# Causal attention: values through stationary tokens, with the probabilities moving and two heads in halves of the columns

## The chip, the cores and the metric

One core of a Trainium2 chip runs the whole computation as one program. The metric is the time of one execution on the device in microseconds, lower is better.

## The reference

The input x is 4 batches of 64 channels by 32x32 positions, so 1024 tokens of 64 channels a batch, all fp32.

```python
# 1. attention over positions with 32 channels, softmax over all 1024 keys, and a residual
att = softmax(einsum('bmi,bmj->bij', k, q)); x = x + wo @ (att @ v)
# 2. causal attention with 8 heads of width 64 on t = tokens(x), after a layer norm, and a residual
scores = q @ k.T / 8 ; scores[above the diagonal] = -1e30
t = t + concat_heads(softmax(scores) @ (ln(t) @ Wv)) @ Wo
# 3. a recurrence over the 1024 tokens, on batch-normalised W @ ln(t), and a residual
y[t] = sigmoid(wx[t] + V @ y[t-1]);  t = t + y
```

The change is in part 2 alone.

## The kernel before

**Units and items.** Part 1 is 4 units (one a batch), part 2 is 16 units of two heads (4 batches by 4 pairs of heads). A unit of part 2 has 9 pairs of items, `ATTN_RUNS`; the two items of a pair are the two heads. An item is 512 columns of transposed scores: keys of one 128-token tile on the partitions, queries in the columns, in one or two runs `(key tile, first query tile, query tiles, place)`. The 9 pairs cover the lower triangle of the causal matrix: pairs 1, 2 and 8 have two runs, the others one. Eight blocks of a unit lie on the diagonal and need the mask: one in pairs 0 and 7, two in pairs 1, 2 and 8.

**One item.** TensorE makes the scores of both heads, each on 64 rows of the array, as three fp16 products (keys and queries are split into a high and a low fp16 part), into one of 3 PSUM banks a head (`ST`). ACT writes exp of them as fp32 (`probs`, ring of 10) and, for a split item, once more as fp16 (`probs_high`). POOL subtracts for `probs_low`. Three pairs later TensorE multiplies with the values: the 128x128 block of probabilities is stationary and 65 columns of values move (64 channels of the projected output and a one, which sums the denominator). A split item takes three fp16 products for each block (L574, L576, L578), a whole item one fp32 product (L570). Every sixth item is whole (`ATTN_WHOLE`), 3 of 18.

**Values and scale.** The values are tokens times a matrix of Wv and Wo, so a product with them gives the head's share of the output at once. Each unit computes them in two "values" steps: 8 small products each, two ACT casts, one DVE subtraction. When a half of the queries (4 tiles) of a head is complete, DVE takes the reciprocal of the denominators (L979) and scales (L983), and POOL adds to the tokens (L1260): 4 times a unit.

**Row maxima.** The scores are made shift-free by the row maxima of a cheaper score (high parts alone), computed one unit ahead: one product a head and step (L497), masks by a product of an identity and a mask (L483), a DVE reduction (L903), a transpose, a negation (L927) and a DMA into the queries' first row.

**Order.** Every engine is in order and walks the same slots: item i is scored in slot i, and its pair in an even slot. Value products come `LAG` = 6 slots later, that is three pairs. Within a slot TensorE does value products, then the auxiliary products of the slot (`AUXES`: queries, values, max transpose, keys), then masks, maxima and scores. DVE does scales, reductions, then the subtractions of the auxiliary products, then pieces of layer norms. From slot 64 on all auxiliary products use one PSUM bank, and the maxima two (one a head), so each waits for the user before it. Scores of a pair wait until the first head of the pair before has both its exponentials. Layer norms of a batch run on POOL (`pool_ln1`, L1286 to L1291, with Newton steps L1271 to L1274 ahead) at fixed slots.

## Time and profile before

| | |
|---|---|
| median of 3 runs | 571.24 us |
| lowest and highest | 567.42 and 571.98 us |
| profiled execution, first to last instruction | 567.0 us |
| PE, DVE, ACT, POOL busy | 490.0, 398.8, 429.3, 424.4 us |
| mean granted TensorE clock | 0.974 |

The profile is one execution, seen by the hardware profiler; its span lies 0.4 us under the lowest of the three runs. Busy time of PE counts each matmul with its latency, so close matmuls overlap in it. "Idle before" is the time in which an engine stood still ahead of an instruction, with what ended it.

### The profile page before, as it was taken

The numbers are of one execution on the slowest core, as the hardware profiler recorded it, in microseconds if no ns is written. First come the engines' busy times: TensorE is split into PE (matmuls) and PEld (weight loads), VectorE is DVE, ScalarE is ACT, GpSimd is POOL, SyncE is SP. The second block draws the span as 40 slices with busy tenths as digits, with TensorE's granted clock in tenths as the row PEclk, the third lists the DMA queues.
The fourth block names the chain that finished last, engine by engine and source line by source line (L and its number), as shares of the span: only waits on it lengthen the run. The fifth ranks groups of instructions, "written<-read, shape, count | busy, mean of one in ns | idle before, by whom it ended". The sixth has DMA issues, their size and how long they took to land.

```text
span 567.0 us, 16744 instructions
## 1 busy us (share of the span) xinstructions
PE 490.0 (86%) x6771; PEld 323.0 (57%) x6771; DVE 398.8 (70%) x909; ACT 429.3 (76%) x832; POOL 424.4 (75%) x463
## 2 busy tenths in 40 slices
PE   4699978988799998889999988998999999787783
PEld 1277655655565755565666756565666766564431
DVE  5878888767678786576767676766767786328757
ACT  3488867866778878587888878787888878785593
POOL 3867965857988797968788797899788799985002
PEclk9999999989999999799999999999999999998698
DMA  9100000000000000000000000000000000000001
GB/s 230 68 3 2 2 20 1 4 1 3 1 22 2 3 3 2 3 1 21 2 3 2 4 3 1 21 3 1 1 3 3 2 3 2 2 2 2 0 2 74
DMA packets 3580, 7.46 MB, mean 13 GB/s; under 512 B 1168, under 2 KB 1456, under 8 KB 3376
## 3 DMA queue, kind: packets, MB, share of 16 engines
q1 hardware_dynamic: 3056, 5.34, 3.5%
q8 instruction: 54, 0.88, 0.7%
q10 hardware_dynamic: 448, 1.05, 0.6%
q14 instruction: 22, 0.18, 0.1%
HBM read 4.22 MB, written 1.05 MB: 9 GB/s over the span
## 4 chain that ended last, share of the span: by engine, by line
PE 45%; DVE 22%; POOL 17%; ACT 9%; issue 6%; DMA 1%; DVEq 0%; SPq 0%; POOLq 0%; ACTq 0%
POOL probs_low L1250 10%; PE bank L537 9%; DVE attn_partial_max L903 7%; ACT probs_high L779 6%; PE bank L497 6%; PE bank L570 5%; PE bank L574 4%; DVE conv_partial_max L897 3%; PE bank L578 3%; PE bank L576 3%; PE bank L455 2%; PE bank L522 2%; PE bank L483 2%; PE bank L456 2%; POOL tokens L1260 2%
## 5 line engine op out<-in xcount | busy, mean ns | idle before, releaser
L1250 POOL TENSOR_TENSOR probs_low<-probs,probs_high 128x512 f16<-128x512 f32 x288 | 327.6, 1158 | 77.5 <-ACT probs_high L779 76.7
L775 ACT ACTIVATE probs<-bank 128x512 f32<-128x512 f32 x352 | 214.7, 611 | 84.2 <-PE bank L537 69.0
L903 DVE TENSOR_REDUCE attn_partial_max<-bank 128x1 f32<-128x512 f32 (+2 forms) x288 | 185.3, 685 | 99.5 <-PE bank L497 99.0
L779 ACT ACTIVATE probs_high<-bank 128x512 f16<-128x512 f32 x288 | 176.8, 614 | 0.0
L574 PEld LDWEIGHTS bank<-values_high,probs_high 128*128 128x128 f16 x1152 | 105.7, 98 | 74.2 <-issue 35.8
L574 PE MATMUL bank<-values_high,probs_high 128*128 128x65 f16 x1152 | 128.8, 196 | 15.5 <-POOL probs_low L1250 11.4
L576 PE MATMUL bank<-values_low,probs_high 128*128 128x64 f16 x1152 | 127.6, 194 | 0.0
L578 PE MATMUL bank<-values_high,probs_low 128*128 128x65 f16 x1152 | 127.1, 194 | 0.0
L576 PEld LDWEIGHTS bank<-values_low,probs_high 128*128 128x128 f16 x1152 | 106.9, 99 | 3.2
L578 PEld LDWEIGHTS bank<-values_high,probs_low 128*128 128x128 f16 x1152 | 107.2, 98 | 0.0
L570 PE MATMUL bank<-values,probs 128*128 128x65 f32 x512 | 71.7, 278 | 0.8 <-POOL probs_low L1250 0.8
L570 PEld LDWEIGHTS bank<-values,probs 128*128 128x128 f32 x512 | 64.7, 192 | 3.5 <-POOL probs_low L1250 1.0
L497 PE MATMUL bank<-attn_keys_high,queries_high 64*128 64x512 f16 (+3 forms) x384 | 56.7, 332 | 7.9 <-ACT probs_high L779 6.0
L1260 POOL TENSOR_TENSOR tokens<-scaled_outputs,tokens 128x256 f32<-128x256 f32 x71 | 51.7, 729 | 8.0 <-DVE scaled_outputs L983 3.3
L537 PE MATMUL bank<-queries_high,attn_keys_high 64*128 64x512 f16 (+3 forms) x384 | 55.6, 326 | 1.1 <-ACT probs_high L779 1.1
L537 PE MATMUL bank<-queries_high,attn_keys_low 64*128 64x512 f16 (+3 forms) x384 | 55.5, 325 | 0.0
L537 PE MATMUL bank<-queries_low,attn_keys_high 64*128 64x512 f16 (+3 forms) x384 | 55.5, 325 | 0.0
L897 DVE TENSOR_REDUCE conv_partial_max<-bank 128x1 f32<-128x512 f32 x64 | 42.8, 687 | 5.8 <-PE bank L470 4.7
L983 DVE TENSOR_TENSOR scaled_outputs<-bank,reciprocal_denominators 128x256 f32<-128x256 f32 x72 | 30.6, 425 | 7.6 <-DVE reciprocal_denominators L979 0.5
L522 PE MATMUL bank<-causal_masks,identity_bf 128*128 128x128 bf16 x256 | 27.5, 219 | 6.6 <-ACT probs_high L779 6.4
L497 PEld LDWEIGHTS bank<-attn_keys_high,queries_high 64*128 64x128 f16 x384 | 15.3, 93 | 29.7 <-issue 6.8
L1343 POOL TENSOR_TENSOR x_split<-probs 128x512 f32<-128x512 f32 x4 | 4.2, 1092 | 36.1 <-ACT probs L878 36.1
(192 smaller groups left out, 708.9 us busy)
## 6 DMA issues: line engine op xcount, KB each, us to landing
x_channels<-in_x_cm SPq DMA_DIRECT2D x6, 256.0 KB, 7.6
tokens<-in_x_tm SPq DMA_DIRECT2D x1, 1024.0 KB, 10.4
out<-ln_channels SPq DMA_DIRECT2D x4, 256.0 KB, 2.0
attn_weights<-in_attn_w ACTq DMA_DIRECT2D x1, 512.0 KB, 6.2
attn_keys_split<-attn_keys_high SPq DMA_DIRECT2D x4, 128.0 KB, 2.3
attn_keys_split<-attn_keys_low SPq DMA_DIRECT2D x4, 128.0 KB, 2.4
queries_high<-minus_max_rows SPq DMA_DIRECT2D x32, 2.0 KB
x_channels<-in_x_cm ACTq DMA_DIRECT2D x2, 128.0 KB, 3.2
```

Source lines behind the costliest of these rows:

```text
L497: last[r] = nc.tensor.matmul(prep_bank(m + r)[:, at * P:(at + tiles) * P], q[rows(r), t * P:(t + 1) * P], xs_hi[rows(r), b * N + j0 * P:b ...
L537: last[r] = nc.tensor.matmul(ST[(i + r) % ST_RING][:, at * P:(at + tiles) * P], keys[rows(r), b * N + j * P:b * N + (j + 1) * P], queries[ ...
L570: ins = nc.tensor.matmul(dst, e32[:, item % E_RING, cols], v32[v % 2][:, j, r, :], start=opens, stop=True, skip_group_check=True)
L574: nc.tensor.matmul(dst, hi, v_hi[v % 2][:, j, r, :], start=opens, stop=False, skip_group_check=True)
L576: nc.tensor.matmul(dst[:, 0:C], hi, v_lo[v % 2][:, j, r, :], start=False, stop=False, skip_group_check=True)
L578: ins = nc.tensor.matmul(dst, lo, v_hi[v % 2][:, j, r, :], start=False, stop=True, skip_group_check=True)
L775: ins = nc.scalar.activation(e32[:, i % E_RING, :], o[:], ACT.Exp, scale=scale)
L779: ins = nc.scalar.activation(p_hi[:, i % P_RING, :], o[:], ACT.Exp, scale=scale)
L897: nc.vector.reduce_max(cmx[v % 2][:, t, part:part + 1], o[:], AX).then_inc(s_prep_used, 1)
L903: nc.vector.reduce_max(dst, o[:].rearrange("p (n w) -> p n w", n=n), AX).then_inc(s_prep_used, 1)
L1250: nc.gpsimd.tensor_tensor(out=p_lo[:, i % P_RING, :], in0=e32[:, i % E_RING, :], in1=p_hi[:, i % P_RING, :], op=ALU.subtract).then_inc(s_r ...
L1260: nc.gpsimd.tensor_tensor(out=dst, in0=scaled[:, half % S_RING, :, :], in1=dst, op=ALU.add).then_inc(s_added, 1)
```

## The change

The value products change sides. Tokens after the layer norm (`xh`, 64 channels, the first replaced by a one) are stationary, 64 columns for each head, and the probabilities move, up to 512 columns at once. Head 0 writes partitions 0 to 63 of the bank and head 1 partitions 64 to 127 (`sums_bank`): halves of the array's columns. So the products give sums of tokens, not of values. When a half of the queries is complete, ACT casts the sums of both heads to fp16 (`o_hi`), DVE subtracts (`o_lo`), and an auxiliary step "outputs" for each head multiplies them with the value matrix: four tiles of three products, with 64 rows. DVE scales from its bank as before. The "values" steps are gone.

Pairs 3 to 6 are split in fp16; pairs 0, 1, 2, 7 and 8 are whole, for both heads. All masked blocks are in whole pairs; they are now set to zero after the exponential by POOL (`pool_mask`, `affine_select` on the two heads' 128 columns at once), and the score masks on TensorE are gone. The masks of the maxima stay, as two products over half the rows each. Layer-norm steps on POOL get a cast and a subtraction for the tokens' fp16 parts and move by some slots.

```diff
-CONV_WHOLE, ATTN_WHOLE = 4, 6
+CONV_WHOLE = 4
+SPLIT_PAIRS = (3, 4, 5, 6)
...
-ATTN_MAXT_SLOT, ATTN_VALUES_SLOTS = -4, (-2, 2)
+ATTN_MAXT_SLOT, OUTPUT_SLOTS, LAST_OUTPUT_SLOTS = -4, (12, 16, 24, 28), (12, 14, 24, 25)
...
-LN1_APPLY_SLOT = (23, 80, 136, 214)
-KEY_SLOTS = ((32, 34), (88, 92), (154, 160), (226, 232))
+LN1_APPLY_SLOT = (23, 80, 144, 216)
+KEY_SLOTS = ((32, 34), (89, 93), (157, 161), (227, 231))
...
+        def pe_sums(i):
+            v = unit_of(i)
+            b = batch_of(v)
+            if not whole(i):
+                nc.tensor.wait_ge(s_rest, rests(i + 1))
+            elif diagonals(i):
+                nc.tensor.wait_ge(s_masked, masked(i))
+            else:
+                nc.tensor.wait_ge(s_probs, i + 2)
+            last = [None, None]
+            for j, t0, tiles, at in runs_of(i):
+                c = t0 // TPC
+                opens = (v, c) not in OPENED
+                if opens:
+                    OPENED.add((v, c))
+                    if v > B:
+                        nc.tensor.wait_ge(s_sums, 2 * (v - B - 1) + c + 1)
...
+                if whole(i):
+                    products = ((xh[b % 2][:, j, 0, :], e32, E_RING),)
+                else:
+                    x_hi, x_lo = xh_hi[b % 2][:, j, :], xh_lo[b % 2][:, j, :]
+                    products = ((x_hi, p_hi, P_RING), (x_lo, p_hi, P_RING), (x_hi, p_lo, P_RING))
+                for n, (x, p, ring) in enumerate(products):
+                    for r in range(2):
+                        last[r] = nc.tensor.matmul(sums_bank(c)[rows(r), cols], x, p[:, (i + r) % ring, src],
+                                                   start=opens and n == 0, stop=n == len(products) - 1,
+                                                   skip_group_check=True)
...
+            elif what == "outputs":
+                n, r = k // 2, k % 2
+                h = 2 * (n // NC % PAIRS) + r
+                nc.tensor.wait_ge(s_sums, n + 1)
+                for t in range(TPC):
+                    o, cols = bank[:, t * PO:(t + 1) * PO], slice(t * P, (t + 1) * P)
+                    hi, lo = o_hi[n % 2][rows(r), cols], o_lo[n % 2][rows(r), cols]
+                    nc.tensor.matmul(o, hi, pr_hi[rows(r), h, :], start=True, stop=False, skip_group_check=True)
+                    nc.tensor.matmul(o[:, 0:C], hi, pr_lo[rows(r), h, :], start=False, stop=False,
+                                     skip_group_check=True)
+                    ins = nc.tensor.matmul(o, lo, pr_hi[rows(r), h, :], start=False, stop=True,
+                                           skip_group_check=True)
...
+        def act_sums(n):
+            v, c = B + n // NC, n % NC
+            nc.scalar.wait_ge(s_values, closed_by(v, c) + 1)
+            if n >= 2:
+                nc.scalar.wait_ge(s_aux, AUX_OF["outputs", 2 * (n - 2) + 1] + 1)
+            nc.scalar.activation(o_hi[n % 2][:], sums_bank(c)[:], ACT.Copy).then_inc(s_sums_cast, 1)
...
+        def dve_sums(n):
+            nc.vector.wait_ge(s_sums_cast, n + 1)
+            nc.vector.tensor_tensor(out=o_lo[n % 2][:], in0=sums_bank(n % NC)[:], in1=o_hi[n % 2][:],
+                                    op=ALU.subtract).then_inc(s_sums, 1)
...
+        def pool_mask(i):
+            nc.gpsimd.wait_ge(s_probs, i + 2)
+            for at in diagonals(i):
+                e = e32[:, i % E_RING:i % E_RING + 2, at * P:(at + 1) * P]
+                nc.gpsimd.affine_select(out=e, in_=e, pattern=[[0, 2], [1, P]], compare_op=ALU.is_ge, fill=0.0, base=0,
+                                        channel_multiplier=-1).then_inc(s_masked, 1)
```

How the order moves on TensorE, in a late unit, around the queries products and the scores of pair 2. Before, with the values of two items of the pair three steps earlier ahead of them:

```order
L574 MATMUL bank<-values_high,probs_high 128x65
L576 MATMUL bank<-values_low,probs_high 128x64
L578 MATMUL bank<-values_high,probs_low 128x65
...
L570 MATMUL bank<-values,probs 128x65 x4
L455 MATMUL bank<-attn_keys_split,qk_matrix_high 128x512
L456 MATMUL bank<-attn_keys_split,qk_matrix_low 128x512
L522 MATMUL bank<-causal_masks,identity_bf 128x128 x4
L497 MATMUL bank<-attn_keys_high,queries_high 128x512 x2
L537 MATMUL bank<-queries_high,attn_keys_high 128x256 x4
```

Now, the same place and what follows up to the next maxima:

```order
L600 MATMUL bank<-probs,ln_out 64x384 x2
L600 MATMUL bank<-probs,ln_out 64x128 x2
L460 MATMUL bank<-attn_keys_split,qk_matrix_high 128x512
L461 MATMUL bank<-attn_keys_split,qk_matrix_low 128x512
L506 MATMUL bank<-attn_keys_high,queries_high 128x512 x2
L535 MATMUL bank<-queries_high,attn_keys_high 128x256 x4
...
L600 MATMUL bank<-probs,ln_out 64x512 x2
L659 MATMUL bank<-value_matrix_high,sums_high 128x65
L660 MATMUL bank<-value_matrix_low,sums_high 128x64
L662 MATMUL bank<-value_matrix_high,sums_low 128x65
...
L506 MATMUL bank<-attn_keys_high,queries_high 128x512 x2
```

The value products went from 65 to up to 512 moving columns and from one head at a time to two side by side, the score masks (L522) went, and in the next step the outputs stand between the sums and the maxima.

DVE, steps 2 to 6 of a late unit (reductions are of the maxima, `queries_low` are the subtractions of the queries steps). Before:

```order
L903 TENSOR_REDUCE attn_partial_max<-bank 128x4 x2
L959 TENSOR_TENSOR values_low<-bank,values_high 128x512
L979 RECIPROCAL reciprocal_denominators<-bank 128x4
L983 TENSOR_TENSOR scaled_outputs<-bank,reciprocal_denominators 128x256
L979 RECIPROCAL reciprocal_denominators<-bank 128x4
L983 TENSOR_TENSOR scaled_outputs<-bank,reciprocal_denominators 128x256
L903 TENSOR_REDUCE attn_partial_max<-bank 128x1 x2
L964 TENSOR_TENSOR queries_low<-bank,queries_high 128x512
L903 TENSOR_REDUCE attn_partial_max<-bank 128x1 x4
```

Now:

```order
L937 TENSOR_REDUCE attn_partial_max<-bank 128x1 x2
L1026 TENSOR_TENSOR sums_low<-bank,sums_high 128x512
L994 TENSOR_TENSOR queries_low<-bank,queries_high 128x512
L1008 RECIPROCAL reciprocal_denominators<-bank 128x4
L1012 TENSOR_TENSOR scaled_outputs<-bank,reciprocal_denominators 128x256
L937 TENSOR_REDUCE attn_partial_max<-bank 128x1 x4
L994 TENSOR_TENSOR queries_low<-bank,queries_high 128x512
L1008 RECIPROCAL reciprocal_denominators<-bank 128x4
L1012 TENSOR_TENSOR scaled_outputs<-bank,reciprocal_denominators 128x256
L937 TENSOR_REDUCE attn_partial_max<-bank 128x1 x2
L943 TENSOR_REDUCE row_max<-attn_partial_max 128x2x4 x2
L1026 TENSOR_TENSOR sums_low<-bank,sums_high 128x512
```

The two scales of a half no longer stand together, and each subtraction of sums comes behind the reductions of its slot.

POOL, one unit. Before:

```order
L1250 TENSOR_TENSOR probs_low<-probs,probs_high 128x512 x10
L1260 TENSOR_TENSOR tokens<-scaled_outputs,tokens 128x4x64 x2
L1250 TENSOR_TENSOR probs_low<-probs,probs_high 128x512 x5
L1260 TENSOR_TENSOR tokens<-scaled_outputs,tokens 128x4x64 x2
```

Now:

```order
L1299 TENSOR_TENSOR probs_low<-probs,probs_high 128x512 x4
L1321 TENSOR_TENSOR tokens<-scaled_outputs,tokens 128x4x64
L1299 TENSOR_TENSOR probs_low<-probs,probs_high 128x512 x2
L1321 TENSOR_TENSOR tokens<-scaled_outputs,tokens 128x4x64
L1307 AFFINE_SELECT probs<-probs 128x2x128 x3
L1321 TENSOR_TENSOR tokens<-scaled_outputs,tokens 128x4x64
L1307 AFFINE_SELECT probs<-probs 128x2x128 x5
```

Of 15 low parts 8 are left, and 8 masks came.

## Rows read from the trace of the kernel before

**Rows 1.** The page, section 1: busy us (share of the span) and instructions.

```profile
PE 490.0 (86%) x6771; PEld 323.0 (57%) x6771; DVE 398.8 (70%) x909; ACT 429.3 (76%) x832; POOL 424.4 (75%) x463
```

**Rows 2.** Groups by line, whole span: count, busy, mean ns, idle; one instruction.

```profile
L1250 POOL TENSOR_TENSOR probs_low<-probs,probs_high 128x512 f16<-128x512 f32 x288 | 327.6, 1158 | 77.5 <-ACT probs_high L779 76.7
L1260 POOL TENSOR_TENSOR tokens<-scaled_outputs,tokens 128x256 f32<-128x256 f32 x71 | 51.7, 729 | 8.0 <-DVE scaled_outputs L983 3.3 <-POOL tokens L1260 0.4
...
L927 DVE TENSOR_SCALAR minus_max_rows<-bank x16: 269/279/279, 105.9 to 489.2; 16x128 f16<-16x128 f32 x16
```

**Rows 3.** PE timeline, 409 to 425 us: start, length, count, [idle].

```profile
415.18 0.38 PE L537 MATMUL bank<-queries_high,attn_keys_high 64*128 64x512 f16 x2
...
424.12 0.20 PE L574 MATMUL bank<-values_high,probs_high 128*128 128x65 f16 x1
...
424.86 0.22 PE L455 MATMUL bank<-value_matrix_high,attn_keys_split 128*128 128x128 f16 x1
```

**Rows 4.** PE's timeline, 425 to 441 us.

```profile
425.30 0.39 PE L483 MATMUL bank<-causal_masks,identity_bf 128*128 128x128 bf16 x4
425.52 0.39 PE L522 MATMUL bank<-causal_masks,identity_bf 128*128 128x128 bf16 x4
425.84 0.39 PE L497 MATMUL bank<-attn_keys_high,queries_high 64*128 64x128 f16 x4
426.07 0.38 PE L537 MATMUL bank<-queries_high,attn_keys_high 64*128 64x384 f16 x4
426.29 0.38 PE L537 MATMUL bank<-queries_low,attn_keys_high 64*128 64x384 f16 x4
...
426.82 0.20 PE L574 MATMUL bank<-values_high,probs_high 128*128 128x65 f16 x1
...
427.20 1.08 PE L570 MATMUL bank<-values,probs 128*128 128x65 f32 x8
428.21 0.39 PE L455 MATMUL bank<-attn_keys_split,qk_matrix_high 128*128 128x512 f16 x1
...
431.28 0.39 PE L497 MATMUL bank<-attn_keys_high,queries_high 64*128 64x512 f16 x2 [0.43 <-ACT probs_high L779]
...
438.87 0.38 PE L537 MATMUL bank<-queries_high,attn_keys_high 64*128 64x512 f16 x2
```

**Rows 5.** ACT's timeline, 425 to 441 us.

```profile
430.05 0.60 ACT L775 ACTIVATE probs<-bank 128x512 f32<-128x512 f32 x1 [0.34 <-PE bank L537]
430.55 0.59 ACT L779 ACTIVATE probs_high<-bank 128x512 f16<-128x512 f32 x1
```

**Rows 6.** DVE timeline, 216 to 262 us; PE timeline (last row).

```profile
242.92 1.29 DVE L903 TENSOR_REDUCE attn_partial_max<-bank 128x2 f32<-128x512 f32 x2 [1.68 <-PE bank L497]
244.12 0.68 DVE L959 TENSOR_TENSOR values_low<-bank,values_high 128x512 f16<-128x512 f32 x1
...
251.76 0.18 DVE L979 RECIPROCAL reciprocal_denominators<-bank 128x4 f32<-128x4 f32 x1
...
252.38 0.17 DVE L979 RECIPROCAL reciprocal_denominators<-bank 128x4 f32<-128x4 f32 x1
...
244.86 0.66 PE L651 MATMUL bank<-constants,ln_out 128*128 128x128 f32 x4 [0.56 <-DVE values_low L959]
```

**Rows 7.** PE's weight loads, 553 to 567 us.

```profile
555.63 0.19 PEld L752 LDWEIGHTS bank<-probs,ffn_weights 128*128 128x128 f32 x1 [0.24 <-ACT probs L875]
556.05 0.19 PEld L752 LDWEIGHTS bank<-probs,ffn_weights 128*128 128x128 f32 x1 [0.24 <-issue]
```

**Rows 8.** POOL groups and timeline, 205 to 262 us; PE waits.

```profile
L1303 POOL CAST causal_masks<-constants 128x256 bf16<-128x256 f32 x1 | 0.4, 397 | 0.0
...
L1291 POOL COPY ln_out<-ln_out 128x512 f32<-128x512 f32 x4 | 2.4, 611 | 0.3
...
227.12 2.27 POOL L1250 TENSOR_TENSOR probs_low<-probs,probs_high 128x512 f16<-128x512 f32 x2
...
PE bank L574 <- POOL probs_low L1250: 3.4, 2, 3.1
```

More of the change, by code:

```diff
@@ L471, in pe_conv_prep, with pe_mask @@
                              start=True, stop=True).then_inc(s_prep, 1)
+        def pe_mask(blocks, opens):
+            for half in range(2):
+                for r in range(2):
+                    nc.tensor.matmul(blocks[r], masks[rows(r), half, 0, :], masks[rows(r), half, 1, :],
+                                     start=opens and half == 0, stop=False, skip_group_check=True)
         def pe_max_masks(m):
             _, v, k = PREPS[m]
+            if v == B and k == 0:
+                nc.tensor.wait_ge(s_masks, 32)
             for r in range(2):
                 pe_wait_bank(BANK_HAD["prep", m + r])
[L478 to L485 removed]
+            ends = [(at + tiles) * P for t, j0, tiles, at in ATTN_MAXES[k // 2][0] if j0 + tiles - 1 == t]
+            for n, end in enumerate(ends):
+                pe_mask([prep_bank(m + r)[:, end - P:end] for r in range(2)], n == 0)
         def pe_maxes(m):
@@ L839, in _ @@
                     act_aux(m)
+                for n in SUMS_AT.get(g, ()):
+                    act_sums(n)
                 for i in items_at(g):
@@ L1101, in _ @@
             for g in range(FIRST_SLOT, LAST_SLOT):
-                for half in HALVES_AT.get(g, ()):
-                    dve_scale(half)
+                for half in CONV_HALVES_AT.get(g, ()):
+                    dve_conv_scale(half)
                 for m in auxes_at(g):
@@ L1120, in _ @@
                         dve_rowmax(v)
+                for n in SUMS_AT.get(g, ()):
+                    dve_sums(n)
                 for m in auxes_at(g):
@@ L1359, in _ @@
             sp.dma_start(gbt[:], gb).then_inc(s_ffn, 16)
+            sp.wait_ge(s_init, 2)
+            for r in range(2):
+                sp.dma_start(masks[rows(r), 1, :, :], masks[rows(1 - r), 0, :, :]).then_inc(s_masks, 16)
             for m, (_, _, what, k) in enumerate(AUXES):
```

272 lines of the change are left out of this document (129 added, 143 removed).

## The prediction, made before the changed kernel ran

> **What bounds the kernel now.** I read the page first, then one undisturbed unit in the timelines of PE, ACT and DVE, then the waits. The page [rows 1] has PE at 86% and no engine much behind, but a busy PE here counts the latency tail of every matmul, so the answer lies in the steps. I number the nine steps of a unit 0 to 8: step n computes the row maxima for the next unit, the scores of item pair n, and the value products of pair n-3 (of the unit before where n is below 3).
>
> One unit takes 23.69 us, from the scores at 415.18 to the same ones at 438.87 [rows 3, 4]. The whole sequence of 16 units is slower: the max rows, one per unit, stand at 105.9 and 489.2 [rows 2], 25.55 us apart on average, so 15 intervals carry 15 x (25.55 - 23.69) = 28 us of disturbance. Part of it are bursts of POOL work for a layer norm: behind one, after which the low parts go on at 227.12, PE had waited twice for a low part, up to 3.1 us [rows 8].
>
> Inside a unit two things alternate. Where a step has extra products PE simply works through: from the value products at 424.12 over the aux products at 424.86, masks and maxima to the next scores at 426.07 there is no idle time [rows 3, 4]. In plain steps a loop of latencies sets the pace: ACT starts the first head's exponential at 430.05, its fp16 copy at 430.55, which ends at 431.14, and PE, idle for 0.43 us, starts at 431.28 [rows 4, 5]. By the prices below a unit has nine steps of 1.10, values 8.6, queries and values aux 2.0, masks 1.8 and a transpose, together some 22 us of PE work, and under 2 us of such waiting.
>
> **Prices on PE** [rows 3, 4]. A product of 512 columns for both heads, each on its own half of the rows: 426.07 to 426.29, 0.22 us, the two together, since both are through in 0.39 us with the latency (scores: three such, 0.65; maxima: 0.23). A causal mask block for both heads: 0.11 us (two blocks of the maxima from 425.30 to 425.52). A change of shape costs 0.10 us from scores to values (426.07 + 0.65 = 426.72, then 426.82) and some 0.10 to 0.14 back (425.52 + 0.22 = 425.74, then 425.84). Split values of a pair: 24 matmuls of 65 columns, 424.12 to 424.86, 0.74 us, or 0.031 each. A whole item of one head: four fp32 products of 65 columns in eight passes, from 427.20 to the next product at 428.21, 1.0. So a unit's values cost 7.5 x 0.74 + 3 x 1.0 = 8.6 us now. A 512-column fp32 product is two passes, whose weight loads start at 555.63 and 556.05: 0.43 us a pass [rows 7].
>
> **The change part by part.**
> Removed from PE: the score masks, 8 blocks x 0.11 = 0.9 us a unit, and the values aux, 2 x 0.44 (424.86 to 425.30) = 0.9. Added: four outputs aux of 12 matmuls x 0.031 = 0.37, with their start 0.39 each, 1.6 us a unit. The max masks are now two half-height products for each head, side by side: 0.11 us a block, unchanged.
> The value products themselves: a split pair becomes three fp16 products of 512 columns for two heads, which lie in halves of the array's columns. No row shows column halves at once. If they overlap as the row halves do, 3 x 0.22 = 0.65 us (now 0.74); if not, 1.3. A whole pair is one fp32 product for each head, and each is two passes. In program order these are head 0 first pass, head 0 second, head 1 first, head 1 second. The second can't start before the first has left the same half; the third can run beside the second; the fourth waits for the third. That is three pass times, 1.29 us; with two runs of 384 and 128 columns 1.17, of 256 and 256 1.07. Bounds: 0.86 if the heads overlap wholly, 1.72 if not at all. I take three passes because every row of PE's timeline starts in program order. The Trainium skill, page "TensorE: Matmul & The Clock Gate", section Part 3, says that matmuls start and end strictly in program order whatever tile they are on. By that rule 1.29 stands and 0.86 falls, which agrees with the order of the starts in this trace.
>
> PE work of a unit after the change: nine steps x 1.10 (scores 0.65, maxima 0.23, shape 0.22) = 9.9; split sums 4 x 0.65 = 2.6; whole sums 2 x 1.29 + 2 x 1.17 + 1.07 = 6.0; queries 2 x 0.57 (two products and one more change of shape) = 1.1; outputs 1.6; max masks 0.9; max transpose 0.15. Sum 22.2 us, as much as now. So PE gains nothing: what the masks and the values aux give back, the outputs and the fp32 passes take.
>
> ACT: 15 items of a unit had a second exponential for the fp16 copy, 8 keep it; 4 value casts go and 2 casts of sums come: 9 activations fewer. At 0.50 us from start to start [rows 5] that is 4.5 us less in a unit. It shortens the loop of latencies (the wait of 0.43 us), but most steps are longer than the loop now, so what is late next is PE itself, and DVE.
>
> POOL: 15 low parts x 1.16 = 17.4 us become 8 x 1.16 = 9.3; the four additions of 0.73 stay [rows 2]. Added are 8 masks of 128x256 in fp32. None is in the trace. Nearest below: a cast of the same size, 0.40 us; nearest above: the low part of 128x512, 1.16 [rows 2, 8]. I take 0.6, near the one-input copy of 512 columns at 0.61. POOL then holds 9.3 + 2.9 + 4.8 = 17 us of a unit, and 21.5 at the upper end: hidden under 24.6 in both cases. It isn't late in the steps either: a mask has three steps before its sums.
>
> DVE: the values-low subtraction turns into one of the sums, 2 x 0.68 for 2 x 0.68, but it now stands between PE and PE. The chain is sums on PE, cast on ACT, subtraction on DVE, outputs on PE, with one step for all of it. DVE does in a step, counted from the start of the maxima: +0.42 first reduce (the maxima's latency; 242.92 in rows 6), two reduces to +1.62 (244.12 - 242.92 = 1.20), each further subtraction 0.60 from start to start and 0.68 to its end; PE starts 0.06 us after that end (244.12 + 0.68 = 244.80, then 244.86) [rows 6]. A scale of one half, reciprocal to next reciprocal, is 251.76 to 252.38, 0.62 us.
> - Step 2 has the sums' and the queries' subtraction: DVE is done at +2.90. PE asks for the bank at step 3 after 0.23 + 0.65 + 0.10 + 1.29 + 0.12 = +2.39. Wait with the start: 0.6 us.
> - Step 4 has the queries' subtraction: +2.37 against +2.17 at step 5. Wait 0.2.
> - Step 5 has the scale of an output ahead of the reduces (they end at +1.99), the two row maxima and then the sums' subtraction, which ends at +2.98; PE asks at step 6 after a split pair, +1.75. Wait 1.3 us. Queued behind it on PE are a mask, the maxima and the scores of step 6, so ACT and DVE get their work later by the same 1.3.
> - Steps 7 and 0 find the two maxima banks still being reduced, since an output's scale went first: 0.1 and 0.15.
> Together 2.35 us, and 22.2 + 2.35 = 24.6 us for a unit, +0.9 on 23.69.
>
> Outside the steady unit: the burst of POOL for a layer norm gains a cast and a subtraction, some 1.7 us (0.6 + 1.16), and moves to step 4, between low parts that PE needs; but POOL has slack in the other steps, and the burst of the third norm falls into mask steps. I put the 28 us at 24. The last unit has no maxima, so no DVE waits, and fewer low parts at its end: -1.5. After the last sums, a cast (0.60) and a subtraction (0.68) and the outputs stand ahead of the scale: +2. The masks' exchange by two DMAs on SP lies at the start of the program, 80 us and more ahead of its first use in part 2; queued behind it is only the first row of maxima of part 1, which isn't ready by then: nothing.
>
> Sum against the profiled execution: 567.0 + 15 x 0.9 - 4 - 1.5 + 2 = 577. The profile is the length of the fastest of three runs (567.4), and their median is 571.2; I add 2 and say 579.
>
> **The rivals.**
> A, the heads overlap wholly in fp32 too (0.86 for a whole pair). Steps 1, 2 and 4 get 0.43, 0.32 and 0.32 shorter; steps 3 and 5 don't, since DVE sets them then (+2.90 and +2.37). A unit is 23.5, and the sum 567.0 - 3 - 4 - 2.5 + 2 = 559.5, so 561. Against it: two passes of one product follow each other in one place.
> B, column halves don't overlap in fp32: 1.72 for a whole pair. Steps 1, 2, 4, 5 grow by 0.43, 0.54, 0.54, 0.44, step 3 is covered by the DVE wait: 26.5 a unit, 577 + 15 x 1.95 = 606, so 608. If fp16 halves don't overlap either, +1.7 a unit more. Decided by whether a second head's pass starts before the first head's ends. The Trainium skill, same page and section, has weight loads overlap running matmuls only when their row group differs, or into a background buffer; column halves share all rows. By the first half of that rule B would be the case; the trace has full-height loads 0.031 us apart under running matmuls, which speaks for the background buffer.
> C, the mask costs POOL far more than a copy. POOL is the bound from (24.6 - 12.2) / 8 = 1.55 us a mask; at 2.3, twice the upper row, a unit is 12.2 + 18.4 = 30.6 and the time 577 + 90 = 667. No row speaks for it; the operation is simply unseen.
> D, the disturbances go with POOL's load: of the 28 us only 10 stay. Then 577 - 14 = 563, so 565. For it: POOL has 7 us less in a unit. Against it: the bursts grow and stand between low parts.
>
> **How the numbers follow.** Forecast 0.42, A 0.25, B 0.15, C 0.08, D 0.10. About 1% is what a measurement of this kernel can tell from no change (its three runs lie 0.8% apart). Faster by over 1% (below 565.5): most of A (0.18), half of D (0.06), the low edge of the forecast (0.03): 0.27. Slower by over 1% (above 577): 0.26 of the forecast, B and C: 0.49. Within: 0.24. The forecast alone reaches from 571 to 588. The range leaves out C, most of B's upper half and the bottom of D with A: 554 to 606.
>
> **What would show each step.** A unit's period, from scores to the same scores: 24.6 (A 23.5, B 26.5). Four fp32 passes of a whole pair within 1.3 us. PE idle ahead of the outputs' products at step 6 for 1.3 us, released by the sums' low part on DVE, and at step 3 for 0.6. POOL below 75% busy with masks of about 0.6 us. ACT at some 60%. The prediction is wrong if passes of the two heads start together, if a column half's weights are waited for, or if the long steps around the layer norms go.

## The result, and the profile after

| | before | after |
|---|---|---|
| median of the runs | 570.7 us (4 runs) | 581.7 us (4 runs, 579.2 to 583.0) |
| profiled execution, first to last instruction | 567.0 us | 578.6 us |
| mean granted TensorE clock | 0.974 | 0.953 |

The ratio is 1.020 with an interval of 1.016 to 1.024: the changed kernel is slower by 2%. The page's busy line and the groups that answer to [rows 1, 2, 8] (busy time and mean ns of one; then idle time ahead, with what ended it):

```profile
PE 468.0 (81%) x4915; PEld 235.2 (41%) x4915; DVE 397.5 (69%) x912; ACT 359.6 (62%) x688; POOL 352.1 (61%) x487
...
L1299 POOL TENSOR_TENSOR probs_low<-probs,probs_high 128x512 f16<-128x512 f32 x176 | 200.0, 1157 | 79.0 <-ACT probs_high L809 77.8
...
L1307 POOL TENSOR_SCALAR_AFFINE_SELECT probs<-probs 128x256 f32<-128x256 f32 x128 | 49.6, 407 | 81.2 <-ACT probs L805 80.9
L600 PE MATMUL bank<-probs,ln_out 128*64 128x384 f32 (+3 forms) x512 | 88.4, 456 | 5.0 <-POOL probs L1307 5.0
```

PE, ACT and POOL all have less busy time than before, DVE nearly the same, and the kernel is longer: no engine's load explains it. The mask costs 0.407 us, as much as the cast of its size.

Next, one late undisturbed unit in PE's timeline (start, length, engine, line, operands; in brackets the idle time ahead). It answers to [rows 3, 4]:

```profile
435.66 1.08 PE L600 MATMUL bank<-probs,ln_out 128*64 128x512 f32 x4
436.67 0.40 PE L482 MATMUL bank<-identity_and_causal_mask 64*128 64x128 bf16 x8
...
442.39 0.20 PE L659 MATMUL bank<-value_matrix_high,sums_high 64*128 64x65 f16 x1 [0.91 <-DVE queries_low L994]
...
447.63 0.20 PE L659 MATMUL bank<-value_matrix_high,sums_high 64*128 64x65 f16 x1 [0.32 <-DVE queries_low L994]
...
449.07 0.41 PE L600 MATMUL bank<-probs_high,ln_out_high 128*64 128x512 f16 x2
449.31 0.38 PE L600 MATMUL bank<-probs_high,ln_out_low 128*64 128x512 f16 x2
449.53 0.38 PE L600 MATMUL bank<-probs_low,ln_out_high 128*64 128x512 f16 x2
...
451.17 0.19 PE L659 MATMUL bank<-value_matrix_high,sums_high 64*128 64x65 f16 x1 [1.26 <-DVE sums_low L1026]
```

A whole pair, four fp32 passes (x4), is over after 1.08 us, latency included, and the next product starts after 1.01: two pass times, not three. Unmerged, the first passes of the two heads start at 435.657 and 435.664, the second at 436.137 and 436.144. The waits for DVE are there, 0.91, 0.32 and 1.26 us. The unit, from the first scores to the same ones, takes 23.68 us, exactly as long as before (23.69).

So the 11.6 us lie outside the steady unit. This table is worked out from the first scores products of each of the 16 units in the two timelines:

| us | before | after |
|---|---|---|
| start to the first scores of part 2 | 111.15 | 112.10 |
| 15 intervals, less 15 steady ones | 29.0 | 38.2 |
| last unit | 18.7 | 15.9 |
| from its last scores to the end | 52.8 | 57.2 |
| units 1, 4, 8, 11 (steady is 23.7) | 27.2, 29.5, 26.0, 23.7 | 34.5, 32.0, 27.4, 28.0 |

Unit 4 shows what a long unit is. On POOL (first fence) the block of operations for one layer norm, the burst, runs from Newton steps to L1355 ahead of the low parts; on PE (second fence) the product behind that wait:

```profile
234.80 0.23 POOL L1332 TENSOR_TENSOR newton_scratch<-ln_rstd,ln_var_eps 128x16 f32<-128x16 f32 x1
...
238.40 1.05 POOL L1348 TENSOR_TENSOR ln_out<-tokens,ln_mean_var 128x512 f32<-128x512 f32 x1
239.53 1.04 POOL L1350 TENSOR_TENSOR ln_out<-ln_out,ln_rstd 128x512 f32<-128x512 f32 x1
240.63 0.11 POOL L1352 MEMSET ln_out<- 128x8 f32 x1
240.80 0.61 POOL L1353 COPY ln_out<-ln_out 128x512 f32<-128x512 f32 x1
241.47 0.61 POOL L1354 CAST ln_out_high<-ln_out 128x512 f16<-128x512 f32 x1
242.17 1.15 POOL L1355 TENSOR_TENSOR ln_out_low<-ln_out,ln_out_high 128x512 f16<-128x512 f32 x1
243.28 2.26 POOL L1299 TENSOR_TENSOR probs_low<-probs,probs_high 128x512 f16<-128x512 f32 x2
```

```profile
245.59 0.64 PE L600 MATMUL bank<-probs_high,ln_out_high 128*64 128x512 f16 x2 [5.87 <-POOL probs_low L1299]
246.02 0.64 PE L600 MATMUL bank<-probs_high,ln_out_low 128*64 128x512 f16 x2
```

The burst is 8.5 us in one piece (234.80 to 243.3), and the two low parts behind it end at 245.54. PE had stood for 5.87 us by then, and its next products start 0.43 us apart instead of 0.24: it runs at the lower of its two clock levels (1.2 GHz). The granted clock is the last column but two in these rows, of a stretch before the wait and one behind it:

```profile
236.00:239.00 3.00, 2.86 (x45) 1.61 (x44) 2.08 (x5) 1.62 (x4) 2.34 (x9) 1.00 0.00 0
245.50:250.00 4.50, 4.41 (x44) 2.81 (x46) 1.65 (x4) 0.07 (x1) 3.99 (x6) 0.50 0.03 5
```

Before, the burst of this layer norm was 6.6 us (220.53 to 227.12) and PE's longest wait behind it 3.1. The burst in unit 8 has no Newton steps: 4.9 us (341.97 to 346.86), and PE waits 2.29.

The clock is a second cost of such waits. In the 15 intervals PE stands at the lower level for 27.3 us, 10.2 before. The run with the burst in three parts, below, has a unit that shows the price: its unit 2 has the program of the run before it and the same idle time of PE (3.4 us), but 6.8 us at the lower level and not none, and takes 27.6 us against 24.7. That is 0.43 us for each us at the lower level. Unit 11 of the changed kernel, with 3.4 us of it, is 1.65 us longer than with none in the last run below; unit 1, with 10.2, is 1.9 us longer than with 3.4 in the run with slots 141 and 213, whose program is the same up to there. By these rates (0.28 to 0.49) the 17 us more at the lower level are worth 5 to 8 of the 9.2 us by which the intervals grew, an estimate.

### The profile page after: what moved, and what is told of

The parts are those of the page before. It is cut to its first block, busy times and chain, and to the rows that moved or that the text cites. A ratio compares the mean times of both kernels' runs of the same rounds, so it can differ in the third digit from the quotient of the medians.

```text
span 578.6 us, 12934 instructions
## 1 busy us (share of the span) xinstructions
PE 468.0 (81%) x4915; PEld 235.2 (41%) x4915; DVE 397.5 (69%) x912; ACT 359.6 (62%) x688; POOL 352.1 (61%) x487
## 4 chain that ended last, share of the span: by engine, by line
PE 44%; DVE 33%; POOL 13%; issue 5%; ACT 4%; DMA 1%; DVEq 0%; SPq 0%; POOLq 0%; ACTq 0%
DVE attn_partial_max L937 13%; PE bank L600 11%; PE bank L535 8%; POOL probs_low L1299 6%; PE bank L506 5%; DVE conv_partial_max L931 3%; DVE queries_low L994 3%; DVE sums_low L1026 3%; DVE scaled_outputs L1012 2%; PE bank L482 2%; PE bank L659 2%; PE bank L460 2%; PE bank L559 2%; PE bank L461 1%; ACT probs_high L809 1%
## 5 line engine op out<-in xcount | busy, mean ns | idle before, releaser
L1299 POOL TENSOR_TENSOR probs_low<-probs,probs_high 128x512 f16<-128x512 f32 x176 | 200.0, 1157 | 79.0 <-ACT probs_high L809 77.8
L809 ACT ACTIVATE probs_high<-bank 128x512 f16<-128x512 f32 x176 | 107.4, 610 | 0.0
L1307 POOL TENSOR_SCALAR_AFFINE_SELECT probs<-probs 128x256 f32<-128x256 f32 x128 | 49.6, 407 | 81.2 <-ACT probs L805 80.9
L600 PE MATMUL bank<-probs,ln_out 128*64 128x384 f32 (+3 forms) x512 | 88.4, 456 | 5.0 <-POOL probs L1307 5.0
L659 PE MATMUL bank<-value_matrix_high,sums_high 64*128 64x65 f16 x256 | 30.8, 195 | 39.4 <-DVE sums_low L1026 22.4
L600 PEld LDWEIGHTS bank<-probs,ln_out 128*64 128x64 f32 x512 | 29.9, 137 | 46.9 <-issue 31.5
L600 PE MATMUL bank<-probs_high,ln_out_high 128*64 128x512 f16 x128 | 27.2, 421 | 12.0 <-POOL probs_low L1299 12.0
L482 PE MATMUL bank<-identity_and_causal_mask 64*128 64x128 bf16 x512 | 32.6, 221 | 2.4 <-DVE attn_partial_max L937 1.6
L506 PEld LDWEIGHTS bank<-attn_keys_high,queries_high 64*128 64x128 f16 x384 | 22.0, 95 | 25.6 <-DVE attn_partial_max L937 13.5
L660 PE MATMUL bank<-value_matrix_low,sums_high 64*128 64x64 f16 x256 | 30.4, 192 | 0.0
L662 PE MATMUL bank<-value_matrix_high,sums_low 64*128 64x65 f16 x256 | 30.4, 193 | 0.0
```

The costliest lines, as they stand in the source:

```text
L482: nc.tensor.matmul(blocks[r], masks[rows(r), half, 0, :], masks[rows(r), half, 1, :], start=opens and half == 0, stop=False, skip_group_ch ...
L506: last[r] = nc.tensor.matmul(prep_bank(m + r)[:, at * P:(at + tiles) * P], q[rows(r), t * P:(t + 1) * P], xs_hi[rows(r), b * N + j0 * P:b ...
L600: last[r] = nc.tensor.matmul(sums_bank(c)[rows(r), cols], x, p[:, (i + r) % ring, src], start=opens and n == 0, stop=n == len(products) - ...
L659: nc.tensor.matmul(o, hi, pr_hi[rows(r), h, :], start=True, stop=False, skip_group_check=True)
L809: ins = nc.scalar.activation(p_hi[:, i % P_RING, :], o[:], ACT.Exp, scale=scale)
L1299: nc.gpsimd.tensor_tensor(out=p_lo[:, i % P_RING, :], in0=e32[:, i % E_RING, :], in1=p_hi[:, i % P_RING, :], op=ALU.subtract).then_inc(s_r ...
```

## Experiments

All of them start from the changed kernel unless another base is named. Ratios are to the kernel before, timed beside them (medians 569.5 to 570.5 us). "Disturbance" is the table's second line, what 15 intervals take over 15 steady units.

**Full width in fp32.** The stationary tokens of whole pairs are 128 columns wide, so the two heads' products use the same columns.

```diff
+                if whole(i):
+                    x = xh[b % 2][:, j, :, :].rearrange("p a c -> p (a c)")
+                    for r in range(2):
+                        last[r] = nc.tensor.matmul(sums_bank(c)[:, cols], x, e32[:, (i + r) % E_RING, src], ...)
```

> The changed kernel with the stationary tokens of a whole pair taken 128 columns wide (both copies), so that each head's fp32 product fills the whole array and the heads can't run side by side. It leaves the two heads' sums of whole pairs added together in both halves, so the outputs are not those of the reference; the number of products and columns streamed is unchanged. Theory (the trace of the changed kernel: passes of the two heads start 7 ns apart, so 0.86 us for a whole pair): four passes in a row, 1.72 us a whole pair; steps 1, 2 and 4 grow by 0.86, step 5 by 0.54 (0.32 of it hides behind DVE), step 3 by nothing (the wait of 0.91 us for DVE covers it). Steady unit 23.68 + 3.1 = 26.8 us, profiled execution near 578.6 + 46 = 625 us. Rival (the value products are not what PE is bound by in these steps): under 600 us.

Measured: 622.5 us, one run; steady unit 26.74. A whole pair on PE:

```profile
464.80 1.99 PE L601 MATMUL bank<-probs,ln_out 128*128 128x512 f32 x4
```

Four passes now take 1.99 us with latency against 1.08. With nothing side by side the unit is 3.05 us longer, close to what rival B's sum gave (26.5 a unit). In the changed kernel the heads do overlap.

**Split products one head after the other.** The three products of head 0, then the three of head 1, in program order.

```diff
-                for n, (x, p, ring) in enumerate(products):
-                    for r in range(2):
+                for r in range(2):
+                    for n, (x, p, ring) in enumerate(products):
```

> The changed kernel with the three fp16 products of a split pair issued for one head and then for the other, not alternating; whole pairs are issued as before. It tells how a pass that can't start holds up one of the other half behind it. If products start strictly in program order (the step of the prediction that gave three pass times for a whole pair), the second product of head 0 holds up head 1: 5 x 0.22 = 1.08 us for a split pair in place of 0.65, step 6 unchanged behind its DVE wait, steps 7, 8 and 0 longer by 0.3 to 0.43: steady unit 24.8, profiled execution near 578.6 + 17 = 596 us. If PE looks ahead and starts head 1's products as soon as its half is free, as the fp32 passes of the changed kernel may show: 0.65 us, no change within 2 us.

Measured: 580.7 us, one run; steady unit 23.69. The same pair as above:

```profile
449.15 0.41 PE L600 MATMUL bank<-probs_high,ln_out_high 128*64 128x512 f16 x2
449.39 0.39 PE L600 MATMUL bank<-probs_high,ln_out_low 128*64 128x512 f16 x2
449.61 0.39 PE L600 MATMUL bank<-probs_low,ln_out_high 128*64 128x512 f16 x2
```

Each line still holds one product of each head (x2) and is no longer than a single one. Head 1's first product, fourth in the program, starts with head 0's first and ahead of head 0's second. The unit and the profiled execution (578.8 us) are those of the changed kernel. So PE doesn't hold a product on one column half behind those of the other half that stand earlier in the program. That is the premise on which the prediction chose three passes, and it is wrong here. The Trainium skill, page "TensorE: Matmul & The Clock Gate", section Part 3, has matmuls start and end strictly in program order; this trace shows otherwise for column halves.

**Outputs at odd slots.** The outputs' steps move by one slot, so that DVE's subtraction of the sums has one step more.

```diff
-ATTN_MAXT_SLOT, OUTPUT_SLOTS, LAST_OUTPUT_SLOTS = -4, (12, 16, 24, 28), (12, 14, 24, 25)
+ATTN_MAXT_SLOT, OUTPUT_SLOTS, LAST_OUTPUT_SLOTS = -4, (13, 17, 25, 29), (12, 14, 24, 25)
```

> The changed kernel with the four outputs steps of a unit one slot later (13, 17, 25, 29 in place of 12, 16, 24, 28), so that they come behind the maxima and scores of their step and ahead of the next sums, and DVE scales outside the reductions' way. Theory (the waits for the sums' and queries' subtraction are real costs of the changed order, 0.91 + 0.32 + 1.26 = 2.5 us in each steady unit): most of them go, a steady unit is 21.3 to 22 us instead of 23.68, and the time some 15 x 2 = 30 us lower, ratio to the changed kernel about 0.95. Rival (the chain over DVE is late wherever PE asks, and the wait only moves to the sums or the max transpose behind it): steady unit within 0.5 us of 23.68, under 8 us in all.

Measured: 574.0 us, ratio 1.007 (1.004 to 1.009). The steady unit is 21.88, so the waits for DVE were real and cost 1.80 us a unit. But the disturbance grew from 38 to 58 us, so most of the 27 us was given back. The list of waits, first of the changed kernel, then with odd slots (total, times, longest):

```profile
PE bank L659 <- DVE sums_low L1026: 22.4, 17, 3.1
PE bank L659 <- DVE queries_low L994: 13.8, 23, 1.0
PE bank L600 <- POOL probs_low L1299: 12.0, 5, 5.9
```

```profile
PE bank L600 <- POOL probs_low L1299: 14.4, 5, 7.3
...
PE bank L638 <- DVE scaled_outputs L1012: 11.6, 13, 2.4
...
PE bank L460 <- DVE scaled_outputs L1012: 5.1, 9, 1.6
...
PE bank L680 <- DVE scaled_outputs L1012: 4.5, 3, 1.9
...
PE bank L659 <- DVE sums_low L1026: 3.1, 1, 3.1
```

The waits for the sums' subtraction are gone but for 3.1 us, those for the queries' are 3.9 in the 15 intervals. The wait for low parts grew by 2.4 us alone. New are the waits for DVE's scale ahead of the max transposes (L638), the queries (L460), the keys (L680) and the outputs: together 24.3 us in the 15 intervals, 0.78 in each steady one. Units without a burst lost most: units 2 and 3 rose from 24.0 and 24.5 to 26.0 and 26.6, with 3.1 and 3.7 us of this wait and 3.4 us each at the lower clock level. Units 1, 4 and 8, where low parts or masks wait for the burst, fell by 1.6, 1.3 and 0.3. So the bursts took a part of what the outputs saved, and new waits for DVE and the clock took more. No run parts the two.

**The burst at other slots.** First, slots 144 and 216 go to 141 and 213, right behind the masks of pair 2.

```diff
-LN1_APPLY_SLOT = (23, 80, 144, 216)
+LN1_APPLY_SLOT = (23, 80, 141, 213)
```

> The changed kernel with POOL's layer-norm bursts of batches 2 and 3 at slots 141 and 213 in place of 144 and 216, ahead of the four split pairs and not among them. Theory (the disturbances are POOL bursts of 8.3 and 4.5 us that stand between low parts, behind which PE waited 5.9 us): low parts start late but later steps catch up, the wait gets 2 to 3 us shorter for batch 2 and 2 us for batch 3: 3 to 5 us in all. Rival (the burst costs its whole surplus wherever it stands, since POOL has no slack before the split pairs): within 1 us of the changed kernel, or slower.

Measured: 576.5 us, ratio 1.009 (1.006 to 1.013); units 4 and 8 at 29.4 and 23.8 (32.0 and 27.4). The 5.2 us are at the top of what the theory expected, but 1.9 of them lie in unit 1, which the edit doesn't touch (it has less time at the lower clock level), and unit 9 rose from 26.6 to 27.7. Then behind the mask of pair 7, `(23, 79, 151, 223)`:

> Base: the changed kernel (581.7 us). POOL's bursts for the layer norms of batches 1, 2 and 3 move from slots 80, 144, 216 to 79, 151, 223, just behind the single mask of pair 7, so that only masks stand behind them, the first of which is wanted four steps later. Theory 'the burst is late where low parts or masks of the next three steps stand behind it': the burst of 8.3 us fits into four steps (some 10 us) with its masks, so the long units of the changed kernel, 34.45 (unit 1), 31.97 (unit 4) and 27.37 (unit 8), lose most of what lies over 23.7 to 24.6 that isn't due to other work: unit 4 to some 24.5 (-7.5), unit 8 to 24 (-3.5), unit 1 (moved by one slot only) by 1 to 2; whole time 568 to 572. Rival 'POOL has no room for a burst in any 24 us stretch (15 of its own and 8.3)': a wait of equal length comes up elsewhere, and the time stays within 3 us of the 576.5 of the kernel with slots 141 and 213.

Measured: 578.5 us, ratio 1.013 (1.009 to 1.017). Units 4 and 8 fall to 24.0 and 23.7 as expected, but units 5 and 9 rise to 32.8 and 31.0: the time is the rival's. My theory had left out one user of the burst:

```profile
249.54 1.08 PE L680 MATMUL bank<-constants,ln_out 128*128 128x128 f32 x4 [3.82 <-POOL ln_out_low L1355]
```

These are the transposes for the keys of the next batch, which in units 5 and 9 stand at step 1 or 0. The wait had only moved. With odd outputs on top:

> The run before (bursts at 79, 151, 223) and the outputs at odd slots (13, 17, 25, 29) together. Odd slots alone took the steady unit from 23.68 to 21.88, but the sequence of 15 intervals gained only 8 us and not 27, because units with a burst or layer-norm work grew. Theory 'the two add up': steady unit 21.88, disturbances those of the run before; 15 x 1.8 = 27 us less than it, whole time some 545. Rival 'with shorter units POOL and DVE, which have the same work to do in less time, take it back': each burst (8.3 us of POOL beside 15 us of its own) makes a unit at least 23.3, each unit with 16 tiles of statistics on DVE stays at 25 or more: some 560 to 565.

Measured: 569.7 us, ratio 0.998 (0.995 to 1.001): steady 21.88, disturbance 50. Against the late bursts alone odd outputs gave 9 us, not 27, and the rival's 560 to 565 was too low as well. It was right that the time is taken back; how much of it by POOL and how much by DVE is open.

**The tail.** In the last unit alone pairs 5 and 6 are whole too.

```diff
-    return ... else n // 2 not in SPLIT_PAIRS
+    return ... else n // 2 not in SPLIT_PAIRS[:2 if unit_of(i) == UNITS - 1 else 4]
```

> Base: the changed kernel. In the last unit alone pairs 5 and 6 are whole in fp32 too, so POOL has four low parts fewer (4 x 1.16 us) just before the end, and ACT four copies fewer. Theory 'the longer tail (57.2 us from the last scores to the end, before 52.8) is made by low parts ahead of the additions on POOL, for which DVE's last statistics wait, and behind which the subtraction of the last sums stands on DVE': the addition comes some 2.3 to 3 us sooner, the subtraction starts when the cast is done, the tail is some 54, whole time 2 to 4 us less (578 to 580). Rival 'the tail is the added chain of cast, subtraction and outputs alone': it stays at 57 and the time within 1 us; the two pairs cost PE 0.2 us each more in fp32.

Measured: 581.2 us, ratio 1.019 (1.015 to 1.022): no difference to be told. DVE's timeline of the changed kernel near the end, then with this edit:

```profile
525.29 0.61 DVE L1115 BATCH_NORM_STATS2 ln_stats<-tokens 128x6 f32<-128x64 f32 x4 [4.68 <-POOL tokens L1321]
...
529.37 0.68 DVE L1026 TENSOR_TENSOR sums_low<-bank,sums_high 128x512 f16<-128x512 f32 x1
```

```profile
523.61 0.61 DVE L1115 BATCH_NORM_STATS2 ln_stats<-tokens 128x6 f32<-128x64 f32 x4 [2.13 <-POOL tokens L1321]
...
527.79 0.68 DVE L1026 TENSOR_TENSOR sums_low<-bank,sums_high 128x512 f16<-128x512 f32 x1
```

The last sums' subtraction stands behind 4 us of statistics on DVE, and those wait for an addition on POOL that stands behind low parts. Fewer low parts bring both forward, until the mask ahead of the addition sets it, for which POOL waits 1.65 us for ACT: the tail is 55.8 us instead of 57.2. That part of the theory is seen in the trace, but 1.4 us is less than half of what I expected and below what the three rounds can tell.

**All moves together**: late bursts, odd outputs, the last unit, and the second projection for part 3 out of unit 11.

```diff
-LN3_TRANSPOSE_SLOTS, WX_SLOTS = (257, 263), (261, 267)
+LN3_TRANSPOSE_SLOTS, WX_SLOTS = (257, 263), (261, 281)
```

> All moves together: bursts at 79, 151, 223, outputs at odd slots, the second of the two projections of the layer-norm tokens of part 3 from slot 267 to 281 (between the two queries steps it had waited 1.9 us for DVE in unit 11), and pairs 5 and 6 of the last unit whole. By the theory that each move acts in its own place: the time of the run with late bursts and odd slots less 3 to 4 us for unit 11 (27.97 us in the changed kernel) and 2 to 4 for the tail, 540 if those two add up, and under the kernel before (570.5) by 5%. By the rival that POOL and DVE take it back: 555 to 560, under it by 2 to 3%.

Measured: 565.0 us, ratio 0.990 (0.987 to 0.993). Unit 11 goes from 25.1 to 22.5 and unit 12 from 21.9 to 22.9: 1.6 us from the projection. The time misses both expectations (540, and 555 to 560). Units 1, 5 and 9, with the keys behind the burst, still take 31.2, 32.8 and 32.2.

**Keys later.** Base: all moves.

```diff
-KEY_SLOTS = ((32, 34), (89, 93), (157, 161), (227, 231))
+KEY_SLOTS = ((32, 34), (91, 97), (163, 169), (235, 241))
```

> Base: the run with all moves (565.0 us). There a burst of POOL of 8 to 10 us was still followed by one wait of PE of the same kind, now for the tokens after the norm: the transposes for the keys of the next batch stood at step 1 of the following unit (slots 89, 157, 227), the trace has PE idle for 3.8 to 4.9 us ahead of them, and step 1 or 0 of units 1, 5 and 9 at 6.84, 10.02 and 8.11 us. Here the keys steps of batches 1 to 3 move from (89, 93), (157, 161), (227, 231) to (91, 97), (163, 169), (235, 241). Theory 'the keys alone held the late burst': unit 1 31.2 to 27, unit 5 32.8 to 26, unit 9 32.2 to 26; 4 + 6 + 6 = 16 us less, whole time 547 to 551, 4% under the kernel before. Rival 'POOL has no room': masks or low parts behind the burst are late instead, and the time stays over 560.

Measured: 558.4 us, ratio 0.979 (0.976 to 0.982). 7 us of the 16: unit 9 lost 3.8, unit 3 1.5, unit 1 1.0, unit 5 nothing (32.9). What took the keys' place:

```profile
143.93 1.98 PE L600 MATMUL bank<-probs,ln_out 128*64 128x384 f32 x8 [3.66 <-POOL probs L1307]
...
247.76 1.98 PE L600 MATMUL bank<-probs,ln_out 128*64 128x384 f32 x8 [5.52 <-POOL probs L1307]
...
342.74 1.08 PE L600 MATMUL bank<-probs,ln_out 128*64 128x384 f32 x8 [1.93 <-POOL probs L1307]
```

Now the masks of pair 8 were late. The rival of this run ("masks or low parts behind the burst are late instead") had the mechanism, though the time fell to 558; neither range holds it. The same with the outputs at even slots:

> The run with late keys, but with the outputs back at the changed kernel's slots (12, 16, 24, 28). In the changed kernel the odd slots gained 1.80 us in a steady unit and only some 8 us over all of 15 intervals. Theory 'the rest was hidden behind waits for the bursts and for the keys, which set those units whatever the outputs do': with these waits gone odd slots are worth more, some 15 to 20 us, and this run takes 565 to 570. Rival 'units with layer-norm work on DVE can't gain from odd slots at all': the difference stays at 8 to 9 us, and this run takes 556 to 560.

Measured: 574.0 us, ratio 1.006 (1.004 to 1.008). Odd outputs are now worth 15.6 us, where they were worth 8 and 9. The difference is within the theory's 15 to 20, the time above both its range and the rival's. In the units with a burst or keys (1, 4, 5, 8, 9) odd outputs saved 3.1 us in all on the changed kernel and 8.7 here: so much had been hidden. Another 2.7 us come from units 2 and 3, which here have no time at the lower clock level. Some 11 of the 27 us stay lost, with 21.5 us of waits for DVE's scale in the intervals.

**The burst in three parts.** Base: keys later. The same instructions, with other POOL work between; the Newton steps of batch 2 also come 12 slots sooner (batch 3 has none).

```diff
-LN1_APPLY_SLOT = (23, 79, 151, 223)
+LN1_PART_SLOTS = ((23, 23, 23), (79, 81, 85), (139, 153, 157), (211, 225, 229))
...
-                    if g == LN1_APPLY_SLOT[b]:
-                        pool_ln1(b)
+                    for part in range(3):
+                        if g == LN1_PART_SLOTS[b][part]:
+                            pool_ln1(b, part)
```

> Base: the run with late keys (558.4 us). In it the burst of one layer norm, 8.5 us in one piece, still holds PE at step 1 of units 1, 5 and 9 (7.75, 9.63, 5.15 us, PE idle 3.66, 5.52 and 1.93 us ahead of the sums of pair 8, for its masks). In every placement so far (slots 80/144/216, 141/213, 79/151/223) some product of PE waited 4 to 6 us for what stood behind the piece. Here the same instructions run in three parts with masks and low parts between: Newton steps (3.6 us) at slots 79, 139, 211, the two operations of the norm (2.3 us) at 81, 153, 225, copy, cast and low part (2.5 us) at 85, 157, 229. Theory 'one piece of 8 us exceeds the slack of a mask or low part (three steps, 7 us, less the time POOL is behind), parts under 4 us don't': units 1, 5 and 9 lose their waits, 30.2 to 26.5, 32.9 to 27.3, 28.4 to 26.5, and whole time is some 11 us less, 547. Rival 'POOL has no room in these units (15 us of its own, 8.5 of burst, units of 22 to 24)': the waits spread over several steps, the three units stay at 29 or more, and the time stays over 555.

Measured: 545.4 us, ratio 0.956 (0.953 to 0.958). Units 1, 5, 9 are at 24.5, 25.8 and 25.8 (30.2, 32.9, 28.4). Units 2 and 3 rose, from 24.7 and 25.1 to 27.6 and 26.6, with the same waits but 6.8 and 3.4 us at the lower clock level. Unit 2, the run before and this one:

```profile
167.43:192.14 24.71, 21.27 (x239) 9.73 (x239) 19.80 (x52) 15.58 (x30) 14.77 (x21) 1.00 0.04 10
```

```profile
162.85:190.47 27.62, 24.20 (x239) 10.43 (x238) 19.80 (x52) 15.66 (x30) 14.77 (x21) 0.88 0.04 9
```

POOL's timeline at the second and third part, where masks (L1307) run between them:

```profile
239.60 1.05 POOL L1357 TENSOR_TENSOR ln_out<-tokens,ln_mean_var 128x512 f32<-128x512 f32 x1
240.73 1.04 POOL L1359 TENSOR_TENSOR ln_out<-ln_out,ln_rstd 128x512 f32<-128x512 f32 x1
241.84 0.11 POOL L1361 MEMSET ln_out<- 128x8 f32 x1
242.02 0.41 POOL L1307 TENSOR_SCALAR_AFFINE_SELECT probs<-probs 128x256 f32<-128x256 f32 x1
...
243.23 0.77 POOL L1307 TENSOR_SCALAR_AFFINE_SELECT probs<-probs 128x256 f32<-128x256 f32 x2
243.95 0.61 POOL L1348 COPY ln_out<-ln_out 128x512 f32<-128x512 f32 x1
```

In this run's list of waits PE waits for masks no more, and for low parts of part 2 for 3.5 us in all:

```profile
PE bank L600 <- POOL probs_low L1299: 3.5, 3, 1.5
```

Last, parts and late keys alone on the changed kernel:

> The changed kernel (581.7 us) with nothing but the three parts of the burst (slots 79/81/85, 139/153/157, 211/225/229) and, which they need, the late keys (91, 97), (163, 169), (235, 241); outputs, projections and last unit as in the changed kernel. Theory 'the burst in one piece made most of what the changed kernel's sequence lost over its steady unit': units 1, 4, 5, 8 and 9 go from 34.45, 31.97, 27.83, 27.37, 26.61 to some 27, 24, 27, 23.7, 27 (what is left is the keys' own work of some 3 us), 19 us less, whole time 562 to 564, under the kernel before (570) by 1 to 1.5%. Rival 'the parts only paid together with odd outputs, whose waits stood in the same steps': units 5 and 9 keep 29 or more, whole time over 569.

Measured: 566.0 us, ratio 0.993 (0.991 to 0.996). Units 1, 4, 5, 8, 9 are at 27.5, 24.1, 27.7, 23.7, 27.7, the disturbance 19.0 instead of 38.2. The rival fell. The time at the lower clock level in these intervals fell too, from 27.3 to 1.4 us, so the 19.2 us are waits and clock together. The start, the last unit and the tail gave 4 us back, and 566 is 2 us over the expected interval. Against the run above, odd outputs, projection and last unit are worth 20.6 us here, 14.7 of it in the intervals: with the burst in parts too the loop's 27 us don't come in full.

## Why the prediction was right in its time and wrong in its way

The time, 581.7, lies near the forecast of 579 and within its range, and the sign was right. The way there was not the one described; two errors cancelled.

- **The whole pair at three pass times: wrong.** The step "I take three passes because every row of PE's timeline starts in program order" failed. The pair takes two pass times (1.01 us to the next product), as rival A had it, and its unit of 23.5 is near the measured 23.68. Rows in program order with nothing to overtake said nothing on whether PE could overtake. The forecast's 24.6 put 13.5 us too much into 15 intervals, and the disturbances below 13.2 too little. Full width showed the price of no overlap; heads in turn showed that products of the other half pass by.
- **The waits for DVE: right.** Predicted 0.6, 0.2 and 1.3 us at steps 3, 5 and 6, measured 0.91, 0.32, 1.26. The first two are longer because the pair ahead is shorter, which rival A's sum had said of them. Odd slots took 1.80 us a unit away.
- **Masks and load of POOL: right, on the cheap side.** 0.407 us against a guess of 0.6, at the lower bound. POOL is busy 61%. Rival C fell.
- **Disturbances 28 to 24 us: wrong, in sign.** They went to 38.2. The step counted POOL's load ("POOL has slack in the other steps"), and the burst's two new operations at 1.7 us, which was their size (0.61 and 1.15). What counts is the piece and what stands behind it: 8.5 us on POOL, against some three steps (7 us) between the exponential and its sums; but 4.9 us in unit 8 made PE wait too. Splitting the piece and moving the keys took half of the 38 us away. The sum also had no term for PE's clock: the mean granted clock fell from 0.974 to 0.953, and by the estimate above 5 to 8 us of the growth are this. How much of the growth from 29 is owed to the two operations and how much to the place was not told apart; a burst without them was not tried. Rival D had the sign of a load, and fell too.
- **Unit 11** was in no step of the prediction: the projection waited 1.9 us for DVE's queries subtraction. Moving it, with all else, gave 1.6 us net. The unit grew by 4.3 us (23.7 to 28.0), of which 1.65 is the clock.
- **Last unit -1.5, tail +2:** measured -2.8 and +4.4. The tail's step left out what stands ahead of the subtraction on DVE, the statistics, and of those on POOL, the low parts.

Had the whole pair been taken right and all else kept, the forecast would have been some 565, and the median 17 us over it: rival A's unit came true and its time did not.

## What to carry to other kernels

- A steady stretch tells what a change does to the loop. What surrounds it, work in one piece on an engine that is 61% busy, has to be costed by the length of the piece against the slack of whoever stands behind it, not by the engine's load. Moving such a piece moves the wait to the next user (low parts, keys, masks, in that order here); cutting it in three removed it, for 13 us.
- A gain inside the loop (1.8 us a unit) showed at 8 to 9 of 27 us, and at 16 with the keys moved. The piece hid a part of it, new waits for DVE in units without a piece took more. Read the length and the waits of every unit, not the total alone.
- A wait can cost more than its idle time: where PE stood at the lower clock level behind it, the same work took longer (27.6 us against 24.7 in one unit). Read the granted clock beside the waits before a unit's growth is put down to them.
- Whether an in-order engine may overtake can't be read from a trace in which it had no occasion to.

## What the runs showed of the hardware

Two fp32 products on separate column halves of TensorE run side by side: four passes in 1.08 us with latency, against 1.99 at full width. So do fp16 products even if one head's three stand ahead of the other's in the program: 0.41 us for a pair of them. `affine_select` on POOL on 128x256 fp32 takes 0.407 us, 0.77 for two in a row, as much as a cast of that size. After 5.87 us of idle time PE's 512-column fp16 products started 0.43 us apart rather than 0.24, at a granted clock of 0.50. A unit with the same program and the same idle time of PE took 24.71 us at a granted clock of 1.00 and 27.62 at 0.88.
